# All five instruction lists of a macaron block placed anew, with scores and mixed sums in any free PSUM bank

## The chip, the cores and the metric

The kernel runs on one core of a Trainium2 chip. The metric is the device time of one execution in microseconds (us); lower is better. Engines: PE is TensorE (PEld its weight loads), DVE is VectorE, ACT is ScalarE, POOL is GpSimd, SP is SyncE, which here only issues DMAs.

## The reference

x has shape (4, 512, 128), 2048 rows of 128. There are 8 heads of 16, blocks of 32 rows, and a hidden layer of 512.

```python
x = x + 0.5 * ffn(layernorm(x), W1, b1, W2, b2)
x = x + attn(layernorm(x), w_qkv, w_out, b_out, proj)
x = x + 0.5 * ffn(layernorm(x), W1, b1, W2, b2)

ffn(h)  = relu(h @ W1 + b1) @ W2 + b2
attn(h): q, k, v = split(h @ w_qkv.T)           # 8 heads, blocks of 32 rows
         qp = elu(q @ proj[head]) + 1           # 16 -> 128 features
         kp = elu(k @ proj[head]) + 1
         num = qp @ (kp.T @ v);  den = qp @ kp.sum(rows) + 1e-8   # within a block
         return (num / den) @ w_out.T + b_out
```

## The kernel before

**Tiles and stages.** The rows are four chunks of 512 (four tiles of 128 rows). A unit is the part of a chunk that a stage takes at once, written (chunk, first tile, tiles). `EARLY` (first FFN and LayerNorm of the attention) has five units, chunk 0 in two halves; `LATE` (second FFN) has five, chunk 3 in two halves. k = 0, 1, 2 counts the LayerNorms, f = 0, 1 the FFNs.

A unit goes through: `norm_stats` on DVE (L758, L762, L765, L766), `reciprocal_root` on POOL (a power, L977), `norm_apply` on DVE (L777) or POOL (L989), tile by tile; `turn_normed` on PE (transposes, L277) into a PSUM bank; for an FFN, `normed_hi` on ACT (L601) and `normed_lo` on DVE (L783) split it into two rounded halves. Four times i: `up_high` (L286, L287: two matmuls) and `up_low` (L294) add into one bank, `relu` on ACT (L610), `ffn_down` on PE (L302) adds into one bank. The residuals on DVE are `ffn_a_residual` (L823), `attn_residual` (L840), `ffn_b_residual` (L853). POOL adds the biases beforehand (`add_bias` L993, `add_b2` L1027).

For the attention, `normed_copy` (ACT, L605) takes the turned LayerNorm; `qk_product` (L308, g = 0, 1: four heads each) gives q and k, `qk_hi_copy` (ACT, L616) and `qk_lo_part` (DVE, L789) split them, and SP's `move_qk` spreads them by three DMAs per half (L213) into `qk_packed`, beside constant ones that `move_ones` (L239) has put there. `v_product` (L312), `v_copy` (L621) and `spread_v` (POOL, L1036, four steps) make block-diagonal v.

Then head by head, n = 0 to 31: `feature_product(n)` (PE, L323) writes the PSUM pair `wide[n % 2]` (two banks), `exp(n)` (ACT, L625) reads it, `feature(n)` (DVE, L794) reads both and frees it. In pairs of heads m: `score` (64 small matmuls, L332), `scores_copy` (ACT, L630), `mix` (L340), `divide` (DVE, L804, L806, L809). Once per chunk: `turn_attn` (L369), `attn_copy` (ACT, L634), `out_product` (L377).

**PSUM.** Eight banks: the two `wide` pairs (as single banks W0A, W0B, W1A, W1B outside the features), `SO`, and three general ones, GA, GB, GC. `S`, the scores of a pair, is the first half of `SO`; `O`, the mixed sums, is the second. So `mix_pair(m)` waits for `attn_ready` m, and `divide(m)` also for `scores_out` m + 2.

**The order.** Each engine runs its own list in order; nothing overtakes. In the middle the lists are loops over pairs with fillings by hand between (`fill_0` to `fill_3`, one per chunk, on PE, ACT and DVE):

```python
def episode(m):                      # PE
    wait(pe, feat_ready, 2 * m + 2)
    if m + 1 < NPAIRS:
        feature_product(2 * m + 2)
        feature_product(2 * m + 3)
    if m:
        mix_pair(m - 1)
    score(2 * m)
    score(2 * m + 1).then_inc(scored, 1)
```

A filling is a whole step: four `i` of `ffn_down`, four transposes of `turn_normed`, four steps of `spread_v`. `out_product(2)` and the downs of unit 1 of the second FFN stand behind the last feature product; `turn_normed(2, 2)` stands ahead of the last `mix_pair`. At the start DVE sets `proj_rows` to one (L904) as its first operation, ahead of everything else, since the loads of proj (`load_proj`, L235) write into it. Ten warm-up matmuls (L496) precede PE's list. ACT's first activation is `minus_one` (L697). SP's list is x units 0 and 1 (L230), w_qkv, W2, x unit 2, b2, w_out, x units 3 and 4, proj, b_out, two moves of ones, the moves of q and k, and the stores (L227).

Of the kernel before, what the change touches and what calls it, by code (L numbers as in the profile page):

```python
# [7 lines left out]
ALU = mybir.AluOpType  # L8
# [24 lines left out]
WARMUP = 10  # L33
# [10 lines left out]
def macaron_kernel(nc, x, w_qkv, w_out, b_out, proj, W1, b1, W2, b2, out):  # L44
# [3 lines left out]
    with ExitStack() as ctx:  # L48
# [62 lines left out]
        S = SO[:, 0:2 * P]  # L111
        O = SO[:, 2 * P:2 * P + 2 * NB * VW]
# [9 lines left out]
        ident_set = sem("ident_set")  # L122
        masks_set = sem("masks_set")
        w1_hi_ready = sem("w1_hi_ready")
# [68 lines left out]

        def wait_normed(eng, k, u, done):
# [5 lines left out]
        def wait_all_normed(eng, k, units):  # L200

            wait(eng, xn_on_dve[k], sum(UNITS[k][i][2] for i in range(units) if i in ON_DVE[k]))
            wait(eng, xn_on_pool[k], sum(UNITS[k][i][2] for i in range(units) if i not in ON_DVE[k]))
# [5 lines left out]
        def _(sp):  # L209
            def move_qk(c):  # L210

                def spread_rows(source, g, term):
                    sp.dma_start(qk_packed[term::TERMS, c % 2, g * HALF:(g + 1) * HALF, :].bitcast(F32),  # L213
                                 source[:, g, :].bitcast(F32)).then_inc(qk_moved[g], 16)

                wait(sp, feat_sum, HEADS * (c - 1))
                for g in range(2):
                    wait(sp, qk_hi_ready, 2 * c + g + 1)
                    spread_rows(qk_hi, g, HI_HI)
                    spread_rows(qk_hi, g, HI_LO)  # L220
                    wait(sp, qk_lo_ready, 2 * c + g + 1)
                    spread_rows(qk_lo, g, LO_HI)
# [9 lines left out]
            def load_proj(half):  # L232
                for term in (HI_HI, LO_HI, HI_LO):
                    first = half * KROWS + term
                    sp.dma_start(proj_rows[first:(half + 1) * KROWS:TERMS, :, :],  # L235
                                 proj.rearrange("h d f -> d h f")).then_inc(w_loaded[W_PROJ], 16)

            def move_ones(slot):
                sp.dma_start(qk_packed[ONE::TERMS, slot, :, :].bitcast(F32),  # L239
# [5 lines left out]
            sp.dma_start(wqkv_rows[:, :, :], w_qkv.rearrange("(s r) d -> r s d", s=3)).then_inc(w_loaded[W_QKV], 16)  # L245
            sp.dma_start(w2[:, :, :], W2.rearrange("(i p) d -> p i d", p=P)).then_inc(w_loaded[W_W2], 16)
            load_x(2)
            sp.dma_start(b2_bc[:, :], b2.rearrange("(a d) -> a d", a=1).broadcast_to([P, D])).then_inc(w_loaded[W_B2], 16)
            sp.dma_start(wout_rows[:, :], w_out).then_inc(w_loaded[W_OUT], 16)
            load_x(3)  # L250
            load_x(4)
            sp.wait_ge(rows_set, 1)
            load_proj(0)
            load_proj(1)
            sp.dma_start(bout_bc[:, :], b_out.rearrange("(a d) -> a d", a=1).broadcast_to([P, D])).then_inc(w_loaded[W_BOUT], 16)
            sp.wait_ge(pool_set, 3)
            move_ones(0)
            move_ones(1)
            move_qk(0)
            move_qk(1)  # L260
            move_qk(2)
            move_qk(3)
            for u in range(len(LATE)):
                store(u)
# [5 lines left out]
        def _(pe):  # L270
            def turn_normed(k, u, bank):

                unit = UNITS[k][u]
                c, t0, n = unit
                for t in range(n):
# [4 lines left out]
            def up_high(f, u, i, bank):  # L280
# [3 lines left out]
                if i == 0:  # L284
                    wait(pe, xn_hi[k], u + 1)
# [823 lines left out]
```

## Time and profile before

| | |
|---|---|
| median of three runs | 146.1 us (144.58 to 146.41) |
| the profiled execution | 146.55 us, of which the span from the first to the last instruction is 144.5 us |
| busy in the span | PE 118.5, PEld 93.8, DVE 94.1, ACT 77.9, POOL 57.7 us |
| granted clock of TensorE, mean | 0.953 of full |

A row of the timeline has its start in us, its duration in us, engine, line, operation, output<-inputs, their shapes, and how many instructions were merged; a bracket at the end gives the idle time of the engine before it and what ended that. Durations of matmuls include their latency and overlap, so the pace is read from start to start. A line L12 is line 12 of the kernel, often that of a helper.

### The profile page before, as it was taken

How to read it: one execution, taken by the hardware profiler on the slowest of the kernel's cores; microseconds unless marked ns; L12 is line 12 of the kernel's file. 1: busy time of each engine (PE TensorE's matmuls, PEld its weight loads, DVE VectorE, ACT ScalarE, POOL GpSimd, SP SyncE). 2: the span in 40 equal slices, each digit the busy share in tenths (PEclk: the TensorE clock that was granted, in tenths of full speed). 3: DMA queues.
4: the chain of work that ended last, by engine and by line, in shares of the span. 5: the costliest groups of instructions: out<-in, count | busy, mean ns of one | idle time of the engine just before them, and what ended most of it. 6: DMA issues, size and time to landing. Idle time of an engine off the chain costs nothing.

```text
span 144.5 us, 4470 instructions
## 1 busy us (share of the span) xinstructions
PE 118.5 (82%) x1889; PEld 93.8 (65%) x1889; DVE 94.1 (65%) x258; ACT 77.9 (54%) x125; POOL 57.7 (40%) x90
## 2 busy tenths in 40 slices
PE   5888989887599797899627998998599869962992
PEld 5776957854288564498415675986458837961991
DVE  3699883384685996774995874798874933038311
ACT  4256472487673789546545598665688110701540
POOL 3319277449980491000099900069500091007000
PEclk9999999999999999999985699999999995999699
DMA  4986920640065000092000065000100020000202
GB/s 120 271 231 100 182 48 0 260 176 0 5 253 187 2 5 5 11 346 82 0 7 7 0 223 217 5 5 25 52 0 5 0 73 5 0 0 0 73 5 73
DMA packets 10651, 11.03 MB, mean 76 GB/s; under 512 B 772, under 2 KB 6920, under 8 KB 10632
## 3 DMA queue, kind: packets, MB, share of 16 engines
q1 hardware_dynamic: 10480, 10.49, 23.4%
q8 instruction: 15, 0.25, 0.7%
q10 hardware_dynamic: 152, 0.26, 0.7%
q14 instruction: 4, 0.03, 0.1%
HBM read 2.36 MB, written 1.05 MB: 24 GB/s over the span
## 4 chain that ended last, share of the span: by engine, by line
PE 34%; DVE 25%; issue 15%; ACT 12%; POOL 9%; DMA 3%; POOLq 1%
PE G L302 9%; DVE stats L758 6%; ACT expo L625 6%; DVE feat L794 6%; PE G L308 4%; POOL rstd L977 3%; ACT hidden L610 3%; DVE mean_var L762 3%; PE G L277 3%; DMA x_in<-in_L_attn_x_dram 3%; PE SO L302 2%; PE wide L323 2%; POOL xn L989 2%; POOL v_blocks L1036 2%; DVE xn L777 2%
## 5 line engine op out<-in xcount | busy, mean ns | idle before, releaser
L794 DVE SCALAR_TENSOR_TENSOR feat<-expo,wide 128x1024 f32<-128x1024 f32 x32 | 37.6, 1217 | 13.6 <-ACT expo L625 13.5
L625 ACT ACTIVATE expo<-wide,minus_one 128x1024 f32<-128x1024 f32 x32 | 33.9, 1114 | 15.4 <-PE wide L323 15.4
L977 POOL TENSOR_TENSOR rstd<-var_eps,minus_half 128x4 f32<-128x4 f32 (+1 forms) x15 | 13.5, 898 | 52.9 <-DVE minus_mean L766 52.9
L302 PE MATMUL G<-w,hidden 128*128 128x128 f32 x192 | 23.3, 277 | 0.0
L302 PEld LDWEIGHTS G<-w,hidden 128*128 128x128 f32 x192 | 22.1, 192 | 0.2
L323 PE MATMUL wide<-qk_packed,proj_packed 64*128 64x512 f32 x64 | 12.2, 460 | 9.8 <-DVE feat L794 9.2
L277 PE MATMUL G<-ident,xn 128*128 128x128 f32 x48 | 11.3, 328 | 7.0 <-DVE xn L777 5.3
L610 ACT ACTIVATE hidden<-G,b_cols 128x512 f32<-128x512 f32 (+1 forms) x22 | 13.7, 667 | 5.0 <-PE G L294 5.0
L1036 POOL TENSOR_SCALAR v_blocks<-v_rows,own_block 128x544 f32<-128x544 f32 x16 | 11.5, 739 | 8.8 <-ACT v_rows L621 8.8
L323 PEld LDWEIGHTS wide<-qk_packed,proj_packed 64*128 64x128 f32 x64 | 5.0, 192 | 15.3 <-DVE feat L794 9.6
L601 ACT CAST xnT_hi<-G 128x512 fp32r<-128x512 f32 (+1 forms) x10 | 5.0, 505 | 16.7 <-PE G L277 16.7
L277 PEld LDWEIGHTS G<-ident,xn 128*128 128x128 f32 x48 | 6.6, 156 | 10.4 <-issue 4.1
L332 PE MATMUL SO<-feat 128*32 128x32 f32 x1024 | 12.9, 201 | 0.0
L332 PEld LDWEIGHTS SO<-feat 128*32 128x32 f32 x1024 | 12.0, 113 | 0.4 <-issue 0.4
L989 POOL TENSOR_SCALAR xn<-x,minus_mean,rstd 128x128 f32<-128x128 f32 x24 | 10.5, 451 | 0.7
L286 PE MATMUL G<-xnT_hi,w_hi 128*128 128x512 f32 (+1 forms) x22 | 9.6, 434 | 1.3 <-ACT hidden L610 1.0
L610 ACT ACTIVATE hidden<-wide,b_cols 128x256 f32<-128x256 f32 (+1 forms) x16 | 7.8, 547 | 4.3 <-PE wide L294 4.3
L993 POOL TENSOR_TENSOR x_bout<-x,bout_bc 128x512 f32<-128x512 f32 x4 | 5.1, 1281 | 11.4 <-DVE x L840 11.4
L783 DVE TENSOR_TENSOR xnT_lo<-G,xnT_hi 128x512 fp32r<-128x512 f32 (+1 forms) x10 | 5.7, 577 | 5.0 <-ACT xnT_hi L601 5.0
L340 PEld LDWEIGHTS SO<-v_blocks,scores_sb 128*32 128x32 f32 x256 | 4.7, 112 | 6.2 <-issue 6.1
L287 PE MATMUL G<-xnT_hi,w_lo 128*128 128x512 f32 (+1 forms) x22 | 8.6, 390 | 0.0
L294 PE MATMUL G<-xnT_lo,w_hi 128*128 128x512 f32 (+1 forms) x22 | 8.4, 395 | 0.1
(96 smaller groups left out, 206.8 us busy)
## 6 DMA issues: line engine op xcount, KB each, us to landing
qk_packed<-qk_hi SPq DMA_DIRECT2D x16, 256.0 KB, 2.6
qk_packed<-qk_lo SPq DMA_DIRECT2D x8, 256.0 KB, 4.3
qk_packed<-sixteenth SPq DMA_DIRECT2D x2, 512.0 KB, 8.1
x_in<-in_L_attn_x_dram SPq DMA_DIRECT2D x3, 256.0 KB, 5.3
out_dram<-x SPq DMA_DIRECT2D x3, 256.0 KB, 2.3
proj_rows<-in_L_attn_proj_dram SPq DMA_DIRECT2D x6, 64.0 KB, 2.8
x_in<-in_L_attn_x_dram SPq DMA_DIRECT2D x2, 128.0 KB, 3.6
w<-in_L_ffn_W_dram ACTq DMA_DIRECT2D x1, 256.0 KB, 3.5
```

What stands on the lines that cost most here:

```text
L277: mm = pe.transpose(bank[:, t * P:(t + 1) * P], xn[k][:, c % 2, t0 + t, :], ident[:, :])
L286: pe.matmul(bank, w1_hi[:, w], xnT_hi[k][:, unit[0] % 2, cols(unit)], start=True, stop=False)
L302: mm = pe.matmul(bank[:, t * D:(t + 1) * D], hidden[f][:, i, (t0 + t) * P:(t0 + t + 1) * P], w2[:, i, :], start=(i == 0 and t == 0), stop= ...
L323: mm = pe.matmul(wide[n % 2][:, s, :], proj_packed[krows, h, :], qk_packed[krows, c % 2, h, :], start=True, stop=True)
L332: mm = pe.matmul(S[j * BLOCK:(j + 1) * BLOCK, first:first + BLOCK], feat[:, n % 4, 1, tok], feat[:, n % 4, 0, tok], start=True, stop=True)
L610: nc.scalar.activation(hidden[f][:, i, cols(unit)], narrow(bank, unit), ACT.Relu, bias=b1_cols[:, i:i + 1]).then_inc(hidden_ready[f], 1)
L625: nc.scalar.activation(expo[:, n % 2, :, :], wide[n % 2][:, :, :], ACT.Exp, bias=minus_one[:, 0:1]).then_inc(exp_done, 1)
L758: bn = nc.vector.bn_stats(stats[k][:, c * NT + t0 + t, :], src[:, t0 + t, :])
L794: nc.vector.scalar_tensor_tensor(out=feat[:, n % 4, :, :], in0=expo[:, n % 2, :, :], scalar=1.0, in1=wide[n % 2][:, :, :], op0=ALU.min, op ...
L977: nc.gpsimd.tensor_tensor(rstd[k][:, at], var_eps[k][:, at], minus_half[:, 0:unit[2]], ALU.pow).then_inc(rstd_ready[k], 1)
L989: nc.gpsimd.tensor_scalar(xn[k][:, c % 2, t, :], src[:, t, :], minus_mean[k][:, col], rstd[k][:, col], ALU.add, ALU.mult).then_inc(xn_on_p ...
L1036: nc.gpsimd.tensor_scalar(v_blocks[:, c % 2, :, j, :], v_rows[:, :, :, :].rearrange("p t h d -> p (t h) d"), own_block[:, j:j + 1], 1.0, A ...
```

## The change

The steps are the same and compute the same; their sizes, the engine of each and the number of matmuls stay (ten warm-ups too). What changes is order, bank and grain:

- PE, ACT, DVE, POOL and SP each get one flat list instead of the loops with fillings. `episode`, `step`, `fill_0` to `fill_3`, `early_norm`, `mid_norm` and `late_norm` go.
- `S` and `O` go. `score_pair(m, bank)`, `scores_copy(m, bank)`, `mix_pair(m, bank)` and `divide(m, bank)` take a bank: SO, GA, GB or GC, and for the last pairs a `wide` bank. A wait ahead of each says that the bank's last reader is done. `mix_pair` no longer waits for `attn_ready` m, nor `divide` for the next pair's `scores_out`.
- `feature_product(n + 2)` waits for `feat_ready` n + 1, its own bank's feature, and is placed alone, not in a pair.
- Up, down and transposes are placed by single i or tile: `up_high` and `up_low` of different i interleave, `ffn_down(f, u, first, end, bank)`, `turn_normed(k, u, first, end, bank)` (its semaphore now counts tiles), `norm_apply` and `spread_v` with a range.
- A move of q and k waits, from chunk 2 on, for the features of its own half instead of the whole chunk.
- At the start, DVE runs `norm_stats(0, 2)` and `(0, 3)` ahead of `w1_low`, and sets `proj_rows` after `norm_stats(0, 4)`; the weights are transposed as PE's third step; ACT's first activation is `normed_hi(0, 0)`, ahead of the rounding of W1.
- At the end, `attn_residual(2)` and its stats stand ahead of the features 30 and 31.

Its core, with the lists cut:

```diff
-        S = SO[:, 0:2 * P]
-        O = SO[:, 2 * P:2 * P + 2 * NB * VW]
...
-            def mix_pair(m):
+            def mix_pair(m, bank):
                 c, p = divmod(m, PAIRS)
                 wait(pe, scores_out, m + 1)
-                wait(pe, attn_ready, m)
...
+            def score_pair(m, bank):
+                wait(pe, feat_ready, 2 * m + 2)
+                score(2 * m, bank)
+                score(2 * m + 1, bank).then_inc(scored, 1)
...
             # PE's list, start
             pe.wait_ge(ident_set, 1)
-            for _ in range(WARMUP):
-                pe.matmul(GC[:, 0:P], ident[:, :], ident[:, :], start=True, stop=True)
-            pe.wait_ge(w_loaded[W_B1], 16)
-            pe.transpose(SO[:, 0:NI], b1_rows[:, :], ident[0:NI, 0:NI]).then_inc(b1_turned, 1)
-            turn_normed(0, 0, GA)
-            turn_normed(0, 1, GB)
+            turn_normed(0, 0, 0, 1, GA)
+            warm_up(GB)
+            turn_weights(GC)
+            for _ in range(2):
+                warm_up(GB)
+            turn_normed(0, 0, 1, 2, GA)
+            turn_normed(0, 1, 0, 1, SO)
...
             # PE's list, around head 12
+            score_pair(4, GB)
+            pe.wait_ge(feat_ready, 11)
+            feature_product(12)
+            pe.wait_ge(hidden_ready[0], 19)
+            out_product(0, GC)
+            pe.wait_ge(attnT_ready, 1)
+            up_high(0, 4, 3, GA)
+            up_low(0, 4, 3, GA)
+            pe.wait_ge(scores_out, 5)
+            turn_normed(1, 3, 0, 4, GB)
+            pe.wait_ge(x2_ready, 1)
+            mix_pair(4, GC)
+            pe.wait_ge(hidden_ready[0], 20)
+            score_pair(5, GA)
+            pe.wait_ge(feat_ready, 12)
+            feature_product(13)
...
             # PE's list, end of the features
+            out_product(2, GB)
+            pe.wait_ge(feat_ready, 29)
+            feature_product(30)
+            pe.wait_ge(feat_ready, 30)
+            feature_product(31)
+            pe.wait_ge(hidden_ready[1], 5)
+            mix_pair(13, GC)
+            pe.wait_ge(scores_out, 14)
+            score_pair(14, GA)
+            ffn_down(1, 0, 3, 4, SO)
...
             # DVE's list, start
-            nc.vector.memset(proj_rows[:, :, :], 1.0).then_inc(rows_set, 1)
...
+            norm_stats(0, 0)
+            norm_stats(0, 1)
+            norm_apply(0, 0, 0, 1)
+            norm_stats(0, 2)
+            norm_apply(0, 0, 1, 2)
+            norm_apply(0, 1, 0, 2)
+            norm_stats(0, 3)
+            w1_low()
+            normed_lo(0, 0, GA)
+            normed_lo(0, 1, SO)
+            norm_stats(0, 4)
+            set_rows()
...
             # DVE's list, end of the features
+            feature(29)
+            attn_residual(2, GB)
+            norm_stats(2, 2)
+            feature(30)
+            feature(31)
+            divide(13, GC)
```

## Rows read from the trace of the kernel before

**Rows 1.** Windows view: stretch, length, busy PE, PEld, DVE, ACT, POOL, clock, DMA share, GB/s

```profile
31.97:112.63 80.66, 67.48 (x1491) 50.59 (x1491) 60.12 (x128) 54.53 (x79) 35.01 (x50) 0.96 0.18 65
```

**Rows 2.** Groups of instructions, that stretch: count | busy, mean ns | idle before, releaser

```profile
L794 DVE SCALAR_TENSOR_TENSOR feat<-expo,wide 128x1024 f32<-128x1024 f32 x32 | 37.6, 1217 | 13.6 <-ACT expo L625 13.5
```

**Rows 3.** Timeline of the features: start, duration, instruction, idle time before

```profile
61.94 2.35 DVE L794 SCALAR_TENSOR_TENSOR feat<-expo,wide 128x1024 f32<-128x1024 f32 x2 [0.33 <-ACT expo L625]
...
76.82 1.22 PE L323 MATMUL wide<-qk_packed,proj_packed 64*128 64x512 f32 x4 [3.71 <-DVE feat L794]
...
98.69 0.73 PE L323 MATMUL wide<-qk_packed,proj_packed 64*128 64x512 f32 x4 [0.42 <-DVE feat L794]
...
99.24 2.12 ACT L625 ACTIVATE expo<-wide,minus_one 128x1024 f32<-128x1024 f32 x2 [1.72 <-PE wide L323]
...
100.39 2.35 DVE L794 SCALAR_TENSOR_TENSOR feat<-expo,wide 128x1024 f32<-128x1024 f32 x2 [0.51 <-ACT expo L625]
...
102.79 0.73 PE L323 MATMUL wide<-qk_packed,proj_packed 64*128 64x512 f32 x4 [1.76 <-DVE feat L794]
...
103.48 0.44 PE L340 MATMUL SO<-v_blocks,scores_sb 128*32 128x68 f32 x16
...
103.72 0.79 PE L332 MATMUL SO<-feat 128*32 128x32 f32 x64
...
111.41 1.22 DVE L794 SCALAR_TENSOR_TENSOR feat<-expo,wide 128x1024 f32<-128x1024 f32 x1
```

**Rows 4.** Timeline of the tail

```profile
117.25 1.53 PE L277 MATMUL G<-ident,xn 128*128 128x128 f32 x4 [0.84 <-POOL xn L989]
...
124.34 3.74 PE L302 MATMUL G<-w,hidden 128*128 128x128 f32 x32
...
127.91 0.28 PE L377 MATMUL wide<-wv_out,attnT 128*128 128x128 f32 x1
...
131.89 0.49 PE L277 MATMUL G<-ident,xn 128*128 128x128 f32 x2 [2.92 <-DVE xn L777]
...
141.81 0.42 DVE L853 SCALAR_TENSOR_TENSOR x<-G,x_b 128x256 f32<-128x256 f32 x1 [1.36 <-PE G L302]
```

**Rows 5.** DMA issues: KB, us from issue to landing

```profile
x_in<-in_L_attn_x_dram SPq DMA_DIRECT2D x1, 256.0 KB, 5.3
...
qk_packed<-qk_lo SPq DMA_DIRECT2D x1, 256.0 KB, 2.5
```

**Rows 6.** The two moves of ones into qk_packed, from issue to landing

```profile
DMA to landing us min/median/max: 7.5/8.1/8.7
```

**Rows 7.** Timeline of SP's queue at the start

```profile
2.76 0.51 SPq L230 DMA_DIRECT2D x_in<-in_L_attn_x_dram  x1
...
5.37 4.58 SPq L235 DMA_DIRECT2D proj_rows<-in_L_attn_proj_dram  x6
...
10.62 1.40 SPq L239 DMA_DIRECT2D qk_packed<-sixteenth  x2
```

**Rows 8.** Timeline of the start

```profile
1.00 0.91 DVE L904 MEMSET proj_rows<- 128x1024 f32 x1 [1.00 <-PEq L1098]
...
1.85 1.28 ACT L697 ACT_TABLE_LOAD   x1 [1.85 <-issue]
...
8.57 0.39 PE L286 MATMUL wide<-xnT_hi,w_hi 128*128 128x256 f32 x1 [0.27 <-DVE w_lo L916]
...
9.10 0.86 DVE L758 BATCH_NORM_STATS2 stats<-x_in 128x6 f32<-128x128 f32 x4
...
13.55 1.34 DVE L766 TENSOR_SCALAR minus_mean<-mean_var 128x4 f32<-128x4 f32 x1
13.59 1.27 POOL L993 TENSOR_TENSOR x_b<-x_in,b_half 128x512 f32<-128x512 f32 x1
```

**Rows 9.** Chain of waits, up matmuls at the tail: start, us, what

```profile
120.68 0.43 PE wide L286
...
123.37 0.23 PE G L286
```

More of the change, by code:

```diff
@@ new lines, in _ @@
+            attn_copy(0, GA)
+            exp(11)
+            exp(12)
+            scores_copy(4, GB)
+            relu(0, 4, 3, GA)
+            normed_copy(3, GB)
+            scores_copy(5, GA)
+            exp(13)
+            qk_hi_copy(2, 0, GB)
+            exp(14)
+            exp(15)
+            qk_hi_copy(2, 1, GC)
+            v_copy(2, GA)
+            scores_copy(6, SO)
+            exp(16)
+            scores_copy(7, SO)
+            exp(17)
+            normed_hi(2, 0, GB)
+            exp(18)
@@ new lines, in _ @@
+            relu(1, 0, 2, GA)
+            normed_hi(2, 1, GC)
+            scores_copy(12, GA)
+            exp(27)
+            exp(28)
+            attn_copy(2, GB)
+            relu(1, 0, 3, GA)
+            exp(29)
+            relu(1, 1, 0, GC)
+            scores_copy(13, GA)
+            exp(30)
+            scores_copy(14, GA)
+            exp(31)
+            scores_copy(15, W1A)
+            relu(1, 1, 1, GB)
+            normed_hi(2, 2, GC)
+            attn_copy(3, GB)
+            relu(1, 1, 2, W0A)
@@ L968, in _ @@
-            ffn_b_residual(4, GC)
+            normed_lo(0, 4, GC)
+            feature(2)
+            feature(3)
+            ffn_a_residual(3, GB)
+            norm_stats(1, 3)
+            feature(4)
+            divide(0, GC)
+            qk_lo_part(1, 0, GA)
+            feature(5)
+            feature(6)
+            qk_lo_part(1, 1, GC)
+            divide(1, GA)
+            feature(7)
+            feature(8)
+            divide(2, GA)
+            divide(3, GB)
+            feature(9)
@@ new lines, in _ @@
+            feature(10)
+            feature(11)
+            attn_residual(0, GC)
+            feature(12)
+            norm_stats(2, 0)
+            divide(4, GC)
+            feature(13)
+            qk_lo_part(2, 0, GB)
+            feature(14)
+            ffn_a_residual(4, SO)
+            norm_stats(1, 4)
+            feature(15)
+            divide(5, GB)
+            qk_lo_part(2, 1, GC)
+            divide(6, GA)
+            feature(16)
+            divide(7, GC)
+            feature(17)
@@ new lines, in _ @@
+            feature(18)
+            normed_lo(2, 0, GB)
+            feature(19)
+            feature(20)
+            qk_lo_part(3, 0, SO)
+            attn_residual(1, GA)
+            divide(8, GB)
+            feature(21)
+            feature(22)
+            norm_stats(2, 1)
+            qk_lo_part(3, 1, GB)
+            feature(23)
+            feature(24)
+            divide(9, GC)
+            divide(10, GB)
+            feature(25)
+            feature(26)
+            divide(11, GB)
@@ new lines, in _ @@
+            normed_lo(2, 1, GC)
+            feature(27)
+            feature(28)
+            divide(12, GB)
+            feature(29)
[4 more added lines that the diff above has]
+            divide(13, GC)
+            divide(14, W0B)
+            ffn_b_residual(0, SO)
+            divide(15, W1B)
+            normed_lo(2, 2, GC)
+            attn_residual(3, GB)
+            norm_stats(2, 3)
+            norm_apply(2, 3, 0, 1)
@@ L971, in _ @@
+            attn_residual(4, GB)
+            norm_apply(2, 3, 1, 2)
+            ffn_b_residual(1, GA)
+            norm_stats(2, 4)
+            normed_lo(2, 3, GB)
+            norm_apply(2, 4, 0, 2)
+            ffn_b_residual(2, W1B)
+            normed_lo(2, 4, W0A)
+            ffn_b_residual(3, GA)
+            ffn_b_residual(4, SO)
         @block.gpsimd
```

1215 lines of the change are left out of this document (689 added, 526 removed).

## The prediction

> **What bounds the kernel now.** I read the stretches first, then the groups of instructions with their idle time, then the timeline. Cut at the first feature (31.97) and at the end of the last one (111.41 + 1.22 = 112.63 [rows 3]), the span has three parts: a start of 31.97 us, 80.66 us of features, and a tail of 31.9 us up to 144.5. In the middle no engine is full: TensorE is busy 67.48, VectorE 60.12, ScalarE 54.53 of 80.66 us [rows 1]. Of VectorE's idle time 13.6 us stand before `feature`, waiting for `exp` [rows 2]; `exp` waits for the feature product, and that for VectorE: a ring. One turn of it stands in [rows 3]: products at 98.69, exp 99.24 (+0.55), feature 100.39 (+1.15), two features of 1.17, next products 102.79: 4.10 us per pair at best. The product of head n+2 needs only feature n (bank n % 2), but `episode` waits for both features and then issues two products. Where work stands between, the ring stops longer: 3.71 us before 76.82 [rows 3]. In the tail it is the order of TensorE's list: the last mix stands behind transposes that wait for POOL (117.25), the out products at 127.91 stand behind a whole unit of downs, and then four microseconds go to a LayerNorm with little beside it (127.91 to 131.89) [rows 4].
>
> **The start.** All waits and durations are those of before; only places change.
> First, VectorE. x unit 2 lands at 2.76 + 5.3 = 8.06 [rows 5, 7]. The new list puts `norm_stats(0,2)` ahead of three of the four first `norm_apply` tiles, `norm_stats(0,3)` after them, and only then `w1_low`. The stats of four tiles begin at 9.10 with 0.86 [rows 8] and take some 1.5 with their three small steps. So 8.1 + 1.55, three tiles at 0.3, stats again 1.55, w1_low 0.65: w1_lo at 12.8 against 8.5. The first up product, 8.57 before [rows 8], comes at about 12.85: 4.3 us later. TensorE also stops at the weight transposes for `w_out`, whose load stands between those of x units 2 and 3; the wait for the second tile of xn, which ends at 10.0, hides it. The ten warm-up products are the same ten, now spread through these holes.
> Next, the constant ones. `proj_rows`' memset (0.91 at 1.00 [rows 8]) goes behind stats(0,4): 12.8 + 0.75 (two lo parts) + 1.55 + 0.9 = 16.0. SP's queue is in order, so the six loads of proj, b_out and both moves of ones follow. Before they ran from 5.37 [rows 7], and the second move of ones, issued at 11.3 in the pair that begins at 10.62 [rows 7], landed 8.7 later [rows 6], at 20.0: 14.65 us in all. Some of that was the x loads in front of them, so I take 13.7: 29.7 (bounds 28.5 and 30.65). The qk moves of chunk 0 stand in the same queue behind them, 768 KB for the first half; in a free queue such a move lands 2.5 us after its issue [rows 5]. Walking TensorE and ScalarE through the new list (down(0,0) complete at 16.9 instead of 15.6, x1 of both half units by 20.4, qk product 0 at 24.0 instead of 23.5, qk_hi 25.6 instead of 25.2) I get TensorE ready for feature product 0 at 30.5. With the moves at 29.7 + about 2.4 = 32.1 it waits 1.6 us more. First feature = 32.1 + 0.54 + 1.15 = 33.8.
> Last, the table load of ScalarE, 1.28 us at 1.85 ahead of its first activation [rows 8]. That activation is now `normed_hi(0,0)`, which stands in the path. If the load runs while the engine waits it costs nothing; if it runs behind the wait, w1_hi is ready at 12.7 instead of 11.4, and w1_low, due at 12.15, starts 0.55 later. The trace can't tell which (its wait was over). I take 0.5, bounds 0 and 1.28. First feature 34.3 against 31.97: **+2.3 us** (bounds 32.2, where the ones don't matter, and 36.5).
> The Trainium skill (ScalarE: Activation LUTs, "Step-by-step: what each stage is for") says that the compiler places the load right before the activation that needs it; the row at 1.85 agrees in place, and by that rule alone the start would be 0.05 us worse than I take it.
>
> **The features.** New are: products placed singly, each waiting for its own feature; scores and mixed sums in GA, GB, GC or SO, whichever is free; fillings cut into single steps between heads. The cost of each operation stays. VectorE's work in the stretch was 60.12; the new list has one `divide` less and `ffn_b_residual(0)` moved behind the last feature (-0.7 -0.7), and one residual with its stats more (+0.7 +1.65): 61.1. That is the floor. The ring for one bank is 0.54 + 1.15 + 1.22 + 0.06 = 2.97 us, and two banks turn at once, so VectorE sees 2.34 of features in 2.97 and has 0.63 over for the rest, which averages (61.1 - 37.6) / 16 = 1.5 a pair. So VectorE should mostly be the bound and not the ring.
> I then walked the five lists head by head with the row durations (an up matmul of 512 columns 0.23 [rows 9], a down step 3.74 / 4 = 0.93 [rows 4], a mixed pair 103.72 - 103.48 = 0.24 and a pair's scores 0.7 to the next start [rows 3], exp 1.06 and feature 1.17 to the next start, qk, v and out product 0.9, which are as many 128-column passes as a down step). VectorE still idles: about 1 us each at features 8 and 9 (score(3) and mix(3) hold the products behind scores_copy), at 13 (product 13 stands behind score(5), which waits for feature 11), around 17 and 25 to 29 (a relu gives its bank late). Feature 12 starts 23.5 us after feature 0 (before 61.94 - 31.97 = 30.0 [rows 3]), features 16, 22 and 28 at 35.5, 46.1 and 58.8, and the last ends at 66.9 (before 80.7). TensorE's list in the stretch is about 57 us at full clock, no bound by itself.
> To the 66.9 I add 2.4 for the shared path of VectorE and POOL: at 13.55 a `minus_mean` of 0.16 took 1.34 while POOL ran the addition that began at 13.59 [rows 8]; eight such additions of 1.28 lie in the stretch, and I count two hits. And 2.7 for 30-odd hand-overs, each under 0.1 us longer than in the walk. Sum 72.0: **-8.7 us** (bounds 64, nearly the floor, and 80.7, where the waits stay).
> The Trainium skill (GPSIMD Engine Reference, "Key points") names that contention: VectorE instructions in a 2-port mode or with two SBUF inputs share their interface with GpSimd. The 32 features have a mean of 1.217 us [rows 2], what they take with POOL idle too, so the trace bears it out for the small ones only; if all of POOL's eight additions hit such a small one, that is 8 x 1.18 = 9.4 us instead of 2.4 and belongs to rival (a).
>
> **The tail.** `attn_residual(2)` with its stats comes two features before the end, so POOL norms unit 2 while the last features run; the last mix no longer stands behind them. From the last feature: scores 0.7, copy 0.4 + 0.15, mix and divide 1.4, transposes and copy 1.2, then two short fillings: out product 3 at +5.3, against 127.91 - 112.63 = +15.3 [rows 4]. In exchange more is left behind it: up(1,2) 2.1, half of down(1,1) 1.8, down(1,2) 3.6 (3.74 at 124.34 [rows 4]), and as before 0.9 + 0.45, ups of units 3 and 4 2.8, downs 3.6. That is 15.3, and the LayerNorm of units 3 and 4 (four us before) has work beside it. The walk ends the last residual's start at +20.5, its end at +20.9. Before, TensorE's clock fell after such waits, to 0.43 us for a product of 0.23 [rows 9], the lower of its two levels (1.2 for 2.4 GHz), for some 1.5 us of loss here and 1.1 at 134; with fewer holes I still leave 1.7. So 22.6 from the last feature to the last residual's end, against 141.81 + 0.42 - 112.63 = 29.6 [rows 4]: **-7.0 us** (bounds 20.5 and 27).
>
> **Sum.** 2.3 - 8.7 - 7.0 = -13.4. The profiled execution took 146.55 (span 144.5), so 133.15; that execution stood 0.45 above the median of the three runs, so 132.7, say **133 us**.
>
> **Rivals.**
> (a) The ring stays. If hand-overs between engines and POOL's additions (7 us more if all of them hit) take back what single products give, the features stay at 80.7 us and only the tail gains: 146.1 + 2.3 - 7.0 = 141.4. For it: TensorE is already busy 67.48 of 80.66 in the stretch [rows 1], and its list has far more waits than before. Against: 13.6 us of idle before features that hang on a wait for the wrong head. 0.17.
> (b) Bank hand-over blocks TensorE: slower. Place: `score_pair` and `mix_pair` in a general bank now wait for that bank's last tenant (a relu, qk_lo, a residual) and the queue is in order, so one late tenant holds the feature products behind it, whose lateness makes the next tenant late. Price: a stop such as the 3.71 us before 76.82 [rows 3] in every other pair instead of twice in all. With the start at 34.3 and the tail at 22.6, the kernel is slower than before as soon as the stretch takes over 85.3 us, 5.3 a pair instead of 5.04. Six stops more than before on the ring: 80.7 + 6 x 3.7 - 8 (the single products elsewhere) = 95, time 156. Against: my walk finds stops of 0.5 to 1.5 us only. 0.07.
> (c) The walk is true as it stands, with no contention and full clock: 66.9 and 20.9, start as taken: 133 - 5.1 - 1.7 = 126. 0.16.
> (d) The table load and the ones cost their upper bounds, and the holes up to 12.85 leave TensorE at its lower clock for the first ups: +2.2 and +1.5 on the forecast, 136.7. For it: TensorE has little but warm-ups between 7 and 12.8. 0.15.
> The forecast itself has 0.45.
>
> **The numbers.** 133, range 124 to 143: it takes in (c), (d) and (a) with two microseconds on the outer sides, and leaves out (b) and what lies under the walk. 2% (2.9 us) is about what a measurement can tell from no change, so faster means less than 143.2. The forecast, (c), (d) and 0.12 of (a) are faster, 0.88; the rest of (a) and the mild end of (b) are within, 0.06; slower 0.06, all of it (b).
>
> **What would show it.** Right: first up near 12.9; ones landing at about 29 to 30 and feature 0 near 34; VectorE idle before `feature` down from 13.6 to some 5; scores and mixes in G banks; the last out products about 5 us behind the last feature. Wrong: `PE <- DVE feat` still 9 us or more; long waits of score or mix for relu or divide; low clock in the tail.

## The result, and the profile after

The changed kernel takes 127.08 us (median of four runs, 126.18 to 127.47) against 146.25 for the kernel before (four runs, 144.58 to 147.15): a ratio of 0.871, interval 0.862 to 0.881. The profiled execution took 127.35 us. The forecast was 133, its range 124 to 143: the time lies inside, on the side of rival (c). Every ratio in this document leaves out executions that lie more than 1.5% above the quickest of the same kernel, while the medians count all of them.

The page of the changed kernel, its busy times, granted clock and costliest groups:

```profile
span 125.5 us, 4517 instructions
PE 112.1 (89%) x1889; PEld 90.0 (72%) x1889; DVE 93.2 (74%) x258; ACT 78.9 (63%) x125; POOL 58.8 (47%) x90
PEclk9999999999999999999999999999999999999999
L1065 DVE SCALAR_TENSOR_TENSOR feat<-expo,wide 128x1024 f32<-128x1024 f32 x32 | 38.1, 1216 | 4.7 <-ACT expo L846 4.6
```

The busy times are nearly those of before; only TensorE's is lower (118.5 then; times the clock of 0.953 that it had in the mean, this is 112.9), since the clock is now full in every slice. For VectorE, busy 93.2 us where it was 94.1, the 19.2 us between the profiled executions are nearly all idle time. Its idle time before `feature` is 4.7 us where it was 13.6 [rows 2]. In the stretch of the features all of its idle time fell from 20.5 us (80.66 less 60.12 [rows 1]) to 5.6 (66.11 less 60.48), so a good third of what was saved did not stand before `feature`: in the kernel before, 3.0 us stood before `qk_lo_part` and 1.7 before `divide`.

The windows view of the changed kernel, its features and its tail (columns as in [rows 1]):

```profile
35.59:101.70 66.11, 63.95 (x1477) 47.57 (x1479) 60.48 (x136) 53.37 (x75) 30.63 (x48) 1.00 0.20 75
101.70:125.50 23.80, 20.90 (x246) 19.13 (x245) 11.50 (x36) 10.05 (x20) 6.03 (x8) 1.00 0.15 45
```

| stretch | before | after | difference | forecast |
|---|---|---|---|---|
| start, to the first feature | 31.97 | 35.61 | +3.6 | +2.3 |
| first feature to the last one's end | 80.66 | 66.1 | -14.5 | -8.7 |
| from there to the last residual's end | 29.6 | 21.5 | -8.1 | -7.0 |

The timeline of the changed kernel at marks of the features and of the tail:

```profile
35.61 2.35 DVE L1065 SCALAR_TENSOR_TENSOR feat<-expo,wide 128x1024 f32<-128x1024 f32 x2 [1.05 <-ACT expo L846]
...
52.42 1.22 DVE L1065 SCALAR_TENSOR_TENSOR feat<-expo,wide 128x1024 f32<-128x1024 f32 x1 [1.45 <-ACT expo L846]
...
59.52 1.22 DVE L1065 SCALAR_TENSOR_TENSOR feat<-expo,wide 128x1024 f32<-128x1024 f32 x1
...
70.81 1.21 DVE L1065 SCALAR_TENSOR_TENSOR feat<-expo,wide 128x1024 f32<-128x1024 f32 x1
...
99.39 2.34 DVE L1065 SCALAR_TENSOR_TENSOR feat<-expo,wide 128x1024 f32<-128x1024 f32 x2
...
103.31 0.44 PE L417 MATMUL wide<-v_blocks,scores_sb 128*32 128x68 f32 x16
...
106.86 0.61 PE L443 MATMUL G<-wv_out,attnT 128*128 128x128 f32 x4
...
111.49 0.59 PE L319 MATMUL G<-ident,xn 128*128 128x128 f32 x2 [0.18 <-DVE x L1106]
...
122.81 0.42 DVE L1117 SCALAR_TENSOR_TENSOR x<-SO,x_b 128x256 f32<-128x256 f32 x1 [1.48 <-PE SO L363]
```

Feature 12 comes 23.9 us after feature 0 (59.52), where 61.94 was 30.0 after it [rows 3]; feature 16 at +35.2. The last end is 101.73. In the tail the last mix (103.31) no longer stands behind transposes that wait for POOL, the first out product of unit 3 (106.86) comes 5.1 us behind the last feature instead of 15.3 [rows 4], and the LayerNorm that had four microseconds to itself (127.91 to 131.89 before [rows 4]) has the downs of unit 2 beside it: TensorE's stop before 111.49 is 0.18 us.

### The profile page after: what moved, and what is told of

Its sections match the earlier page's. It is cut to its first block, busy times and chain, and to the rows that moved or that the text cites. A ratio compares the mean times of both kernels' runs of the same rounds, so it can differ in the third digit from the quotient of the medians.

```text
span 125.5 us, 4517 instructions
## 1 busy us (share of the span) xinstructions
PE 112.1 (89%) x1889; PEld 90.0 (72%) x1889; DVE 93.2 (74%) x258; ACT 78.9 (63%) x125; POOL 58.8 (47%) x90
## 4 chain that ended last, share of the span: by engine, by line
PE 27%; POOL 18%; issue 16%; DVE 15%; DMA 11%; ACT 7%; SPq 3%; POOLq 0%; DVEq 0%; ACTq 0%
DVE feat L1065 7%; DMA qk_packed<-qk_lo 6%; POOL rstd L1273 6%; POOL xn L1289 5%; ACT expo L846 5%; DMA x_in<-in_L_attn_x_dram 5%; PE wide L395 4%; PE SO L363 4%; PE wide L363 3%; POOL v_blocks L1328 2%; PE G L363 2%; DVE stats L1029 2%; POOL x_b L1316 2%; POOL x_bout L1293 2%; PE G L417 2%
## 5 line engine op out<-in xcount | busy, mean ns | idle before, releaser
L1273 POOL TENSOR_TENSOR rstd<-var_eps,minus_half 128x4 f32<-128x4 f32 (+1 forms) x15 | 13.4, 895 | 43.8 <-DVE minus_mean L1037 43.8
L319 PE MATMUL G<-ident,xn 128*128 128x128 f32 x40 | 9.2, 293 | 7.5 <-DVE xn L1048 7.3
L395 PE MATMUL wide<-qk_packed,proj_packed 64*128 64x512 f32 x64 | 13.9, 474 | 1.9 <-DMA qk_packed<-qk_lo 1.7
L363 PEld LDWEIGHTS G<-w,hidden 128*128 128x128 f32 x112 | 14.0, 192 | 1.2 <-issue 0.5
L363 PE MATMUL G<-w,hidden 128*128 128x128 f32 x112 | 14.9, 276 | 0.0
L1328 POOL TENSOR_SCALAR v_blocks<-v_rows,own_block 128x544 f32<-128x544 f32 x16 | 12.5, 791 | 5.0 <-ACT v_rows L841 5.0
L820 ACT CAST xnT_hi<-G 128x512 fp32r<-128x512 f32 (+1 forms) x7 | 3.7, 529 | 13.4 <-PE G L319 13.4
L1289 POOL TENSOR_SCALAR xn<-x,minus_mean,rstd 128x128 f32<-128x128 f32 x24 | 10.7, 455 | 0.5
L363 PEld LDWEIGHTS SO<-w,hidden 128*128 128x128 f32 x80 | 9.7, 191 | 1.3 <-issue 1.1
L363 PE MATMUL SO<-w,hidden 128*128 128x128 f32 x80 | 10.5, 279 | 0.0
L363 PE MATMUL wide<-w,hidden 128*128 128x128 f32 x64 | 8.5, 275 | 0.0
L1316 POOL TENSOR_TENSOR x_b<-x,b_half 128x512 f32<-128x512 f32 (+1 forms) x5 | 5.3, 1062 | 6.3 <-DVE x L1106 6.3
L363 PEld LDWEIGHTS wide<-w,hidden 128*128 128x128 f32 x64 | 7.9, 191 | 0.0
L1048 DVE TENSOR_SCALAR xn<-x,minus_mean,rstd 128x128 f32<-128x128 f32 x8 | 5.4, 706 | 3.0 <-POOL rstd L1273 3.0
```

The lines of the kernel that those rows point to most:

```text
L319: pe.transpose(bank[:, t * P:(t + 1) * P], xn[k][:, c % 2, t0 + t, :], ident[:, :]).then_inc(turned[k], 1)
L363: mm = pe.matmul(bank[:, t * D:(t + 1) * D], hidden[f][:, i, (t0 + t) * P:(t0 + t + 1) * P], w2[:, i, :], start=(i == 0 and t == 0), stop= ...
L395: mm = pe.matmul(wide[n % 2][:, s, :], proj_packed[krows, h, :], qk_packed[krows, c % 2, h, :], start=True, stop=True)
L1273: nc.gpsimd.tensor_tensor(rstd[k][:, at], var_eps[k][:, at], minus_half[:, 0:unit[2]], ALU.pow).then_inc(rstd_ready[k], 1)
L1289: nc.gpsimd.tensor_scalar(xn[k][:, c % 2, t, :], src[:, t, :], minus_mean[k][:, col], rstd[k][:, col], ALU.add, ALU.mult).then_inc(xn_on_p ...
L1316: nc.gpsimd.tensor_tensor(x2_b2[:, c % 2, own(unit), :], x2[:, c % 2, own(unit), :], b2_half[:, :].rearrange("p (a d) -> p a d", a=1).broa ...
```

## The experiments

Times are medians; ratios are to the kernel before, run on the same chip. Times in us of different experiments can come from different chips, so a difference of less than a microsecond between them says little. "Stretch" is first feature to the last one's end, read from each kernel's own profile.

**1. The single products.** In the new kernel the even products wait for both features again:

```diff
-            pe.wait_ge(feat_ready, 1)
+            pe.wait_ge(feat_ready, 2)
             feature_product(2)
...
```

> The changed kernel, but each even feature product waits for both features of the pair before, as it did before the change; order and banks stay. If the ring product - exp - feature is what the change opened, each of the 15 even products comes up to 1.17 us later and VectorE's other work fills only part of it: the stretch of the features grows from 66.1 to 74 to 80 us and the time from 127.1 to 135 to 141. If the gain came from the free banks or from the finer grain of the fillings, the stretch stays within 2 us of 66.1 and the time under 129.5.

158.19 us (six runs, 154.88 to 161.27), ratio 1.060 (1.052 to 1.067), which rests on the three quickest (154.88, 155.53, 156.88): slower than the kernel before, and much slower than the 135 to 141 us expected. Stretch 99.2 us. The waits view of this kernel (engine, line, waited for: us in total, times, longest), and then its windows view:

```profile
PEld wide L395 <- DVE feat L1065: 26.1, 15, 2.8
ACT expo L846 <- PE wide L395: 25.0, 16, 2.9
DVE feat L1065 <- ACT expo L846: 24.3, 19, 1.9
```

```profile
34.50:133.70 99.20, 75.84 (x1473) 55.74 (x1471) 62.11 (x136) 55.08 (x75) 30.93 (x48) 0.86 0.14 50
```

Product, `exp` and feature stop for each other 15 to 19 times, and with the stops goes a granted clock of 0.86 in the stretch, at which TensorE's own work grows from 63.95 to 75.84 us. This execution, at 159.5 us, was one with a low clock even for this kernel (0.913 over its span); the quickest, 154.9, had 0.944. So not all of the 33 us by which the stretch grew belong to the edit: against 127.08 us, the median of the three quickest is 28 us more. The two products of a pair now have fillings between them. That one wait too many costs a turn of the ring and the filling as well is how I read the 15 to 19 stops; no run takes the two apart.

The reverse, single products in the old order, in the kernel before:

```diff
-                wait(pe, feat_ready, 2 * m + 2)
+                wait(pe, feat_ready, 2 * m + 1)
                 if m + 1 < NPAIRS:
                     feature_product(2 * m + 2)
+                wait(pe, feat_ready, 2 * m + 2)
+                if m + 1 < NPAIRS:
                     feature_product(2 * m + 3)
```

> The kernel before, with one edit: the two feature products of a pair each wait for their own bank's feature. If the ring alone carries the gain of the feature stretch (80.7 to 66.1), this gives most of it back, some 8 to 12 us, and the time is 134 to 138. If whole fillings between the pairs and the shared bank for scores and sums hold TensorE anyway, the product's wait is over when TensorE comes to it, and the time is 143 to 146. I put it at 140, since the fillings are over 3 us in half of the pairs.

144.3 us, ratio 0.986 (0.978 to 0.993), stretch 79.4. VectorE waits 10.8 us for `exp` instead of 13.5. The whole-step fillings still stand behind both products. Then also five of these fillings (an up step of two i, a down of four) cut in two, with one half between the two products, their relus moved with them:

```diff
                 if m + 1 < NPAIRS:
                     feature_product(2 * m + 2)
+                between(m)
+                wait(pe, feat_ready, 2 * m + 2)
...
```

> The kernel before with single products (as in the run of that name, 144.3) and five long fillings cut in two, the second half between the two products of the next pair: two of four down steps of units 3 and 4, two of four ups of three units, with their relus between the two exps. Those halves are 1.4 to 1.9 us each. If the length of what stands between products is the cause (grain), each cut saves up to its half, 5 to 8 us together: 137 to 140. If the shared bank holds the ring, less than 2 us come: 142.5 to 144.5.

142.01 us, ratio 0.973 (0.965 to 0.982), stretch 76.9, wait for `exp` 7.8 us in ten stops. So these two edits in the old order bring 3.8 of the 14.5 us. The cuts alone, with products in pairs, were not tried, nor were more cuts than these.

**2. The free banks.** In the new kernel both waits of the shared bank come back. The divide's comes back for three pairs of each chunk's four; at the fourth, in the new lists, the next pair's scores themselves wait for the divide:

```diff
             def mix_pair(m, bank):
                 wait(pe, scores_out, m + 1)
+                wait(pe, attn_ready, m)
...
             def divide(m, bank):
+                if p != 3:
+                    wait(dve, scores_out, min(m + 2, NPAIRS))
```

> The changed kernel with the waits that the shared bank needed: a mixed pair waits for the division of the pair before, and three of four divisions wait for the next pair's scores copy. Banks and order stay. If the ring is the cause, mixed sums and divisions are off it and the time grows by 0 to 2 us (127 to 129). If the free banks are the cause, the divisions wait for scores as before and the time grows by 5 us or more (over 132).

137.85 us, ratio 0.943 (0.937 to 0.949), stretch 75.8. The waits view of this kernel, and then its windows view:

```profile
DVE z L1077 <- ACT scores_sb L852: 11.4, 9, 2.3
PEld G L417 <- issue: 8.8, 12, 2.7
```

```profile
34.60:110.40 75.80, 65.71 (x1473) 48.22 (x1471) 60.62 (x136) 53.84 (x75) 31.68 (x49) 0.98 0.18 65
```

VectorE now idles ahead of the divide as well, 11.4 us in nine stops, while its wait before `feature` is 3.3 us, no more than in the changed kernel. Each wait by itself:

> The changed kernel with one of the two waits of the shared bank: a mixed pair waits for the division of the pair before. Both waits together cost 10.7 us (137.85 against 127.1). In that trace VectorE waited 11.4 us for scores copies ahead of divisions, and TensorE's wait ahead of the mixed sums grew from 4.5 to 8.8. If the division's wait is the cost, this run is 127 to 128.5. If TensorE's is, it is 131 or more.

130.85 us (four runs, 128.93 to 131.44), ratio 0.892 (0.880 to 0.903), which rests on two of them (128.93 and 130.79).

> The changed kernel with the other wait of the shared bank alone: three of four divisions wait for the scores copy of the next pair. If VectorE's place in the queue is what the free banks protect, nearly all of the 10.7 us come back: 136 to 138. If it needs both waits, 129 to 133.

134.69 us, ratio 0.924 (0.916 to 0.933). Against the changed kernel's 0.871 the three ratios mean, at 146.25 us, about +3.0 for the mix, +7.7 for the divide and +10.4 for both together: they add up to within a microsecond. The divide's wait is the dearer; in its profile VectorE stands still ahead of it for 8.2 us in eight stops. That it is dearer because a feature stands behind the divide in VectorE's list is argued, not shown. All three costs hold for the new order, which puts other work between a score and its divide; what free banks would bring in the old order was not tried.

**3. The tail.** `attn_residual(2)` and its stats go back behind the last feature in the new kernel, `out_product(2)` with them:

```diff
-            attn_residual(2, GB)
-            norm_stats(2, 2)
             feature(30)
             feature(31)
+            attn_residual(2, GB)
+            norm_stats(2, 2)
```

> The changed kernel with out product 2, its residual and stats behind the last feature, as before. The features should end about 2.3 us earlier (a residual of 0.7 and stats of 1.65 less), and the norm of unit 2 starts some 3 us later against the last feature. If POOL's norm of that unit holds the transposes ahead of the last mixed sums, the tail (21.5 us) grows by 3 to 4 and the time by 1 to 2 us. If the tail is bound by TensorE's work alone, the tail grows by no more than the 2.3 that the features give, and the time stays at 127.1 within 0.5.

130.14 us, ratio 0.889 (0.884 to 0.895), 3.1 us above the changed kernel, where 1 to 2 had been expected. The stretch stays at 66.1, although VectorE has 2.3 us less to do in it: it idles for them instead (waits for `exp` 7.0 us, not 4.6, with 1.01 and 1.27 before the last features). What follows it grows from 23.8 to 27.6 us. So this residual in its new place costs the stretch nothing: it fills idle time of VectorE in the last turns of the ring. The tail alone, in the kernel before:

```diff
-                    wait(pe, x2_ready, 3)
-                    turn_normed(2, 2, GB)
...
+            turn_attn(3, W1A)
+            wait(pe, x2_ready, 3)
+            turn_normed(2, 2, GB)
+            out_product(3, W1B)
+            out_product(4, SO)
...
-            turn_attn(3, W1A)
...
-            out_product(3, W1B)
-            out_product(4, SO)
```

and the same on ScalarE and VectorE (`attn_copy(3)` and `normed_hi(2, 2)` first, `ffn_b_residual(1)` and `normed_lo(2, 2)` behind `divide(15)`).

> The kernel before with only its tail in the new order: the output product of the last mixed pair and its attention residuals come ahead of up and down of unit 2's last part, whose work then lies beside the LayerNorm that follows. If the tail's gain is its own and needs nothing of the features' order, the stretch from the last feature's end to the end falls from 29.6 us to 23 to 25 us, the first 112.6 us stay as they are, and the time is 139 to 142 us. If the tail's length is set by TensorE's and ScalarE's remaining work and not by the order of the residuals, the stretch stays above 28 us and the time is 144.5 to 147 us.

138.12 us, ratio 0.953 (0.942 to 0.964). The stretch is 80.0, what follows 24.0 us where it was 31.9. The windows view of the kernel before, that of this kernel, and then a stretch of this kernel's TensorE timeline:

```profile
112.63:144.50 31.87, 23.48 (x236) 20.44 (x234) 12.02 (x45) 7.74 (x17) 6.79 (x10) 0.89 0.09 26
```

```profile
112.10:136.10 24.00, 19.55 (x236) 17.82 (x234) 12.00 (x46) 7.55 (x17) 6.81 (x10) 1.00 0.11 34
```

```profile
115.85 0.45 PE L340 MATMUL SO<-v_blocks,scores_sb 128*32 128x68 f32 x16
117.14 0.66 PE L369 MATMUL wide<-ident,attn 128*128 128x128 f32 x4 [0.85 <-DVE attn L808]
117.64 0.65 PE L277 MATMUL G<-ident,xn 128*128 128x128 f32 x4
118.47 0.71 PE L377 MATMUL wide<-wv_out,attnT 128*128 128x128 f32 x4 [0.19 <-ACT attnT L634]
```

The last mix stands at +3.7 us behind the last feature, not at +6.1, the out product at +6.3, not +15.3, and the clock is 1.00 where it was 0.89. Moving a few steps of the old lists, with no free bank and no finer grain, shortens the tail by 7.9 us in the profiles (the ratio of the whole times, 0.953, is some 7 us); the change as a whole shortens it by 8.1. The moves were made together, so how they share the 7.9 us isn't known, nor how much of it is the clock's.

**4. The start.** The new kernel without one block of five of the ten warm-ups, that stands before the transpose of xn's fourth tile:

> The changed kernel without the block of five warm-up matmuls at 10.91, which took 2.28 us for 10 passes while the next transpose, ready at about 10.9, came at 13.03. If they are pure delay, the first up comes about 1.2 us earlier (W1's low part is ready at 12.9) and the time falls by up to 1 us. If they are what brings TensorE to its upper clock, the first ups and downs run at the lower one (0.2 for 0.117 us per matmul of 256 columns), the time rises by 1 to 2 us.

126.93 us (six runs, 125.95 to 127.6), ratio 0.870 (0.863 to 0.877): no difference. First up product 13.66 instead of 14.24, first feature 35.4 instead of 35.6. Yet the five are not idle ballast. Up products of this kernel, and then of the changed one:

```profile
14.87 0.41 PE L344 MATMUL G<-xnT_hi,w_hi 128*128 128x256 f32 x1
15.09 0.41 PE L345 MATMUL G<-xnT_hi,w_lo 128*128 128x256 f32 x1
```

```profile
14.56 0.28 PE L344 MATMUL wide<-xnT_hi,w_hi 128*128 128x256 f32 x1
14.68 0.28 PE L345 MATMUL wide<-xnT_hi,w_lo 128*128 128x256 f32 x1
```

Without the five, the first ups follow one another at 0.21 to 0.22 us, up to 15.73, with them at 0.12. So the first qk product comes at 27.09 instead of 26.77, 13.4 us behind the first up instead of 12.5: what the missing warm-ups give, the slow ups take back.

Then the old order of the first 20 us on all engines (PE, ACT, DVE, POOL), with the new features and tail:

> The changed kernel with the start of before: proj_rows set first, the four xn tiles and W1's low part ahead of the stats of x units 2 to 4, the weights turned after the ups of unit 1, ScalarE rounding W1 first, POOL adding b2 to chunk 0 before the second root. In the changed kernel the first up came at 14.24 against 8.57 before, and the first feature at 35.61 against 31.97. If the new order of VectorE's start is what costs these 3.6 us, the first up comes near 8.7, the first feature at 30.5 to 32.5, and the time falls to 122 to 125. If the first feature hangs on what TensorE still has in its list before the product (its work there is the same), or on the DMA, the feature stays at 34 or later and the time within 1.5 us of 127.

125.98 us, ratio 0.863 (0.855 to 0.870); the interval overlaps that of the changed kernel. First up at 8.49, 5.7 us earlier, but the first feature at 33.6, only 2.0 earlier: TensorE now waits 0.93 and 0.81 us for POOL's tiles of xn at 24.96 and 28.78.

Then the changed kernel with POOL's end alone altered, so that its additions no longer lie beside VectorE's last tiles of xn:

```diff
-            reciprocal_root(2, 3)
             add_b2(2)
+            reciprocal_root(2, 3)
             reciprocal_root(2, 4)
+            pool.wait_ge(xn_on_dve[2], 4)
             add_b2(3)
```

> The changed kernel, POOL's last list only: the addition of b2 for unit 2 ahead of the root of unit 3 (POOL is idle there), those of units 3 and 4 after the last xn tile. In the changed kernel xn took 1.29 us at 109.82 and 1.44 for two tiles at 114.07, 0.34 each where POOL makes no addition. If the clash with POOL is a cost on the path, the last transposes come 0.9 us earlier each and the time falls by 0.5 to 1.3 us. If TensorE has enough other work then, the time stays within 0.3.

126.39 us (six runs, 124.43 to 127.14), some 0.7 below the changed kernel. The ratio, 0.856 (0.845 to 0.867), rests on the two quickest, and its interval overlaps that of the changed kernel: not told apart. In the profile the two tiles of unit 3 take 0.35 and 0.34 us where they took 1.29 and 0.34, and the last residual ends 20.9 us behind the last feature, not 21.5. The old start and this end together, at the start with `norm_stats(0, 4)` right behind the stats of unit 3, and POOL's `add_b2_to_x(1)` ahead of the tiles of unit 4 instead of between them, two such tiles at a time:

> The changed kernel with three edits: the start of before (125.98 alone) with the stats of x unit 4 in the 3 us in which VectorE idled at 12, POOL's root and tiles of that unit 5 us earlier and its additions behind them, and POOL's last list as in the run of the tail. In the run with the start of before TensorE waited 0.93 at 24.96 and 0.81 at 28.78 for those tiles. If those waits are on the way to the first feature, it comes at 32 instead of 33.6, and with 0.6 us from the tail the time is 123.0 to 124.8. If other work takes their place, it is 125 to 126.

123.29 us (six runs, 122.96 to 124.09), ratio 0.848 (0.842 to 0.854). It beats both kernels: first up 8.69, first feature 32.6, stretch 65.6, the rest 23.3 of a span of 121.5 us. Of the 4.0 us in the span, 3.0 are the start's, and the last residual again ends 20.9 us behind the last feature. The intervals of its ratio and the changed kernel's do not touch.

## Why the prediction was right, and where it was off

**The bound.** Right for the new kernel: VectorE is now the bound of the stretch, busy 60.48 of 66.11 us (61.1 had been counted). Of the old kernel less is shown. That the ring with a wait for the wrong head set its stretch is borne out only in part, since the right wait and five cut steps in the old order took 3.8 us off it and not 14.5.

**The features.** The walk was right and what I added to it was not. It gave feature 12 at +23.5, 16 at +35.5, the last end at +66.9; measured +23.9, +35.2 and +66.1. Of the idle times that it foresaw the one at feature 8 is there, 1.45 us before 52.42; feature 9 (54.83) starts right behind the divides, and from 72.98 on no stop before a feature is over 0.4 us. So the walk's single stops were in part other than the real ones, and that its sum came within 0.8 us is in part luck. The step that failed is "To the 66.9 I add 2.4 for the shared path ... And 2.7 for 30-odd hand-overs": both measured nothing that can be seen. The hand-overs were probably in the row durations already, since most of these had been read from start to start. For the shared path I had counted eight additions of POOL in the stretch. These were the old kernel's; the new POOL list runs three of them before the first feature and one behind the last (101.96). The four left are these, in the timeline of POOL of the changed kernel:

```profile
36.19 1.29 POOL L1293 TENSOR_TENSOR x_bout<-x,bout_bc 128x512 f32<-128x512 f32 x1
...
59.69 1.29 POOL L1316 TENSOR_TENSOR x_b<-x,b_half 128x512 f32<-128x512 f32 x1 [6.29 <-DVE x L1106]
...
89.39 1.29 POOL L1293 TENSOR_TENSOR x_bout<-x,bout_bc 128x512 f32<-128x512 f32 x1
...
90.62 1.29 POOL L1316 TENSOR_TENSOR x_b<-x,b_half 128x512 f32<-128x512 f32 x1
```

The first three lie over features (those that begin at 35.61, at 59.52, and the pair that begins at 88.63), and no feature of the 32 takes over 1.223 us (1.210 to 1.223). The fourth lies mostly over the small operations of a divide, and they keep their lengths too, as this one of VectorE, which reads and writes SBUF:

```profile
91.09 0.20 DVE L1076 RECIPROCAL z_inv<-z 128x8 f32<-128x8 f32 x1
```

**The start.** Its sign was right, its size 1.3 us short in this profile, and the path another than I took. I had the ones land at 29.7, TensorE ready at 30.5 and the first product at 32.1, held by the moves. In the profile TensorE is ready only at 33.4, and the moves hold it for 0.45 us more. The timeline of all engines of the changed kernel, in order of time:

```profile
10.91 2.28 PE L323 MATMUL G<-ident 128*128 128x128 f32 x10
12.23 0.69 DVE L1137 TENSOR_TENSOR w_lo<-w,w_hi 128x512 fp32r<-128x512 f32 x1
23.92 1.74 DVE L1048 TENSOR_SCALAR xn<-x,minus_mean,rstd 128x128 f32<-128x128 f32 x2 [0.82 <-POOL rstd L1273]
24.29 2.51 POOL L1293 TENSOR_TENSOR x_b<-x_in,b_half 128x512 f32<-128x512 f32 x2
26.77 1.02 PE L375 MATMUL SO<-xnT,wqk 128*128 128x512 f32 x2
27.83 0.59 ACT L836 CAST qk_hi<-SO 128x512 fp32r<-128x512 f32 x1 [0.44 <-PE SO L375]
28.44 1.84 SPq L223 DMA_DIRECT2D qk_packed<-qk_hi  x2
30.32 0.61 SPq L223 DMA_DIRECT2D qk_packed<-qk_lo  x1
33.87 0.74 PE L395 MATMUL wide<-qk_packed,proj_packed 64*128 64x512 f32 x4 [0.45 <-DMA qk_packed<-qk_lo]
```

`w_lo` is ready at 12.9, as I had it (12.8), but then TensorE is late with its own list: five warm-ups, ten passes, take 0.21 us a pass, and the first up comes at 14.24, not 12.85. Two tiles of xn take 1.74 us, where the pair before them (21.09) took 0.60, beside POOL's additions of 24.29: the contention that I had put into the features. It is not new; in the kernel before, the same two tiles took 1.55 us beside an addition:

```profile
19.90 1.27 POOL L993 TENSOR_TENSOR x_b<-x_in,b_half 128x512 f32<-128x512 f32 x1
19.96 1.55 DVE L777 TENSOR_SCALAR xn<-x,minus_mean,rstd 128x128 f32<-128x128 f32 x2 [0.33 <-POOL rstd L977]
```

These two, 1.4 and 1.1 us, are most of the delay of the first qk product, at 26.77 where I had 24.0. From there to the first feature product TensorE's list takes 6.6 us, near the 6.5 of my walk. SP adds little: its first pair of issues takes 1.84 us (1.25 for the next pair), qk_lo lands about 3.5 us after its issue at 30.32, against 2.5 [rows 5], and that costs the 0.45 us before 33.87.

Six more profiles have this same start: those of the even products, of the three runs on the banks, of the late residual and of POOL's end. In them and in this one the first up comes between 13.16 and 14.61, the first qk product always 12.5 us behind it, and the first feature between 34.5 and 35.6; in five of the six no wait of TensorE for a move is listed before the first feature product. So the start costs 2.5 to 3.6 us over the kernel before, and the profile above is the dearest of them. The first up varies with the block of five warm-ups ahead of it, which begins between 9.88 and 10.91 and takes 1.50 to 2.34 us.

That the second move of ones, issued at 22.6, with at most 9.1 us to landing, is in by about 32 and so not last, is worked out from these and not shown by a wait. The term of 0.5 for the table load was 0; the load ran while the engine waited (its first activation, at 10.90, had waited for TensorE for 7.77 us):

```profile
1.84 1.28 ACT L820 ACT_TABLE_LOAD   x1 [1.84 <-issue]
```

**The tail.** Right in mechanism and size: 21.5 us, between the walk of 20.9 and the 22.6 that I took; the out product at +5.1 for +5.3. The 1.7 us for a falling clock did not come: the granted clock is 1.00. The tail's order in the kernel before shows that this part stands by itself; the residual's early place, which that kernel doesn't have, is worth 3.1 us in the new one.

**The rivals.** (a) and (b) did not come. The experiments on products and banks show that a mechanism like (b)'s is real, though: a wait at the head of TensorE's or VectorE's list costs 3 to 10 us in this order, and with the even products' wait the kernel is slower than before. The rows that spoke against it (stops of 0.5 to 1.5 us in the walk) were the right ones to weigh. (d) had the direction of the start right and the cause wrong: the table load cost nothing, the ones did not come last, and the first ups ran at 0.12 us each. Only without the five warm-ups do they run slowly, and that costs 0.9 us. (c), with 126, is what came, within about 1 us: 66.9 and 20.9 forecast, 66.1 and 21.5 measured. That it came so near is in part luck, since the start was 1.3 us and the tail 0.6 us longer, and the features 0.8 us shorter, than it says. I gave it 0.16, for I put allowances of 5.1 and 1.7 us on a walk that needed neither. By stretches, the forecast had the features 5.8 us and the tail 1.1 us too long and the start 1.3 too short.

**What stays open.** Of the features' 14.5 us, 3.8 are had by single products and cut steps in the old order. Taking either freedom away from the new order costs 9.7 us (banks) or up to 33 us (products, in an execution with a low clock) of stretch, more in sum than the whole gain: the new order is built on them and is bad without them. How the other 10.7 us divide between banks, grain and order was not measured.

## What to carry to other kernels

When an order is written out by hand, walk all in-order lists together with start-to-start durations of the old trace, and add nothing for hand-overs on top. A wait must fit the order: the same wait that costs a microsecond or two in coarse lists costs 28 in a list that places work by the event it removed. Take out the parts that stand alone (here the tail, 7 to 8 us with a few moved lines) before rewriting the rest, and count another engine's contending work in the stretch of the new list, not of the old.

## What the runs showed of the hardware that was not expected

POOL's additions slowed VectorE where a TENSOR_SCALAR read and wrote SBUF (`xn`, `minus_mean`), and neither the features nor the reciprocal of a divide. In the tail of the changed kernel it shows once more, in the timeline of both engines:

```profile
109.76 1.27 POOL L1316 TENSOR_TENSOR x_b<-x,b_half 128x512 f32<-128x512 f32 x1
109.82 1.29 DVE L1048 TENSOR_SCALAR xn<-x,minus_mean,rstd 128x128 f32<-128x128 f32 x1 [0.83 <-POOL rstd L1273]
111.36 0.34 DVE L1048 TENSOR_SCALAR xn<-x,minus_mean,rstd 128x128 f32<-128x128 f32 x1
```

1.29 us for a tile that takes 0.34 alone, while features (SBUF and PSUM in) of 1.22 us beside the same additions stay at 1.22. The Trainium skill (GPSIMD Engine Reference, "Key points") names 2-port modes and two SBUF inputs as what shares GpSimd's interface. These rows agree for the features, which have one input in SBUF and were not slowed; whether `xn` ran in such a mode the trace does not say.

And the ten passes at 10.91 (five warm-ups) went at 0.21 us each, though the page's clock row is full there; the four at 13.25 took 0.61 together, 0.11 from one to the next. Without those five the first ups went at 0.21 to 0.22 us in place of 0.12. Both are about the factor of two between the clock's two levels (1.2 and 2.4 GHz), but the granted clock reads 1.00 in all of these rows, so whether the clock or something else held them stays open.
